# Cross attention: softmax sums taken over keys before the product with the values

## Chip, cores and metric

The program runs on one core of one Trainium2 chip. The metric is the time of one execution on the device in microseconds (us), the median of the runs made; less is better.

## The reference, cut to what matters

The reference is a two-layer network on 2 x 1024 tokens of 256 channels. Two of its parts are cross attentions from the 2048 tokens to 2 x 64 context rows (`ctx_512`), both with 16 heads. The first ("x2" in the kernel) has 32 channels per head:

```
q = einsum('bsc,hcd->bhsd', xn, wq); k = einsum('btc,hcd->bhtd', yn, wk); v = einsum('btc,hcd->bhtd', yn, wv)
a = softmax(einsum('bhsd,bhtd->bhst', q, k) * D ** (-0.5), axis=-1)
o = einsum('bhst,bhtd->bhsd', a, v)
```

The second ("x3") is the same computation with 16 channels per head and biases on q, k and v. Everything else (a self attention, two local attentions, feed-forward parts and a mixture of experts) is outside of the change.

## The kernel before

The program is a sequence of stages, each with its own queues on the engines and a barrier of all engines at its end. Both cross attentions are made by one function, `cross_attention`, which is called with the phase names `x2` and `x3`. It works on 16 tiles of 128 tokens. A tile t passes these steps, and a software pipeline written out by hand (the loops over `it`, one per engine, in each of which the steps stand in a fixed order) decides which steps of which tile stand beside one another:

- `statistics`, `inverse_deviation`, `normalise`, `turn_z`, `inputs`: the layer norm of the tile and its transposition, 10 to 14 tiles ahead. `project` and `queries`: the queries of a group of four tiles, in pieces (4 in x2, 2 in x3), one piece per tile and 6 tiles ahead.
- `score` (TensorE, L1155): all 16 x 64 scores of the 128 tokens into the two banks `sps[t % 2]`. The keys stand in `kblk`, blocked by head.
- `top` (VectorE): the negated maximum over the 64 keys of each head (`nmax`, L983), and the scores less it, written to `prob[:, t % 2, :]` in SBUF (L988).
- `exponent` (ScalarE, L1049): the exponential, in place, 128 x 1024.
- `turn_probs` (TensorE, L1108): eight transpositions of 128 x 128 back into `sps[t % 2]`, so that keys lie on the partitions. `evacuate` (ScalarE, L1044): two copies of 128 x 512 to `pT`.
- `weigh` (TensorE): the product with the values `vblk` into the bank `ops` (L1139), and a product with a matrix `ones` into the bank `dps` (L1143), which gives each head's sum of exponentials, repeated over its channels.
- `outputs` (VectorE): the reciprocal of `dps`, MC x 128 columns wide (512 in x2, 256 in x3, L995), and the product with `ops` into `res` (L998).

In the loops, VectorE's order for an `it` is `outputs(it - 1)`, `top(it + 1)`, `normalise`, `statistics`; ScalarE's is `evacuate(it)`, `exponent(it + 1)`, `inputs`, `queries`; TensorE's is `turn_probs(it)`, `turn_z`, `project`, `weigh(it)`, `score(it + 2)`. `weigh(t)` waits for `out_done` of tile t - 1, since there is one bank `ops`. `score(t)` waits until `evacuate(t - 2)` has emptied the scores' banks.

Of the kernel before, what the change touches and what calls it, by code (L numbers as in the profile page):

```python
# [9 lines left out]
def build(nc, io, out):  # L10
# [6 lines left out]
    ALU = mybir.AluOpType  # L17
# [46 lines left out]
    with stack:  # L64
# [761 lines left out]
        def cross_attention(phase, H, DK, src, res, weights, affine, biases, scale, ahead):  # L826
# [10 lines left out]
            with ExitStack() as c:  # L837
# [8 lines left out]
                vmask = sb(phase + "vmask", [P, 2], F32, c)  # L846
                ones = sb(phase + "ones", [P, 2, DK], F32, c)
                kT = sb(phase + "kT", [P, MC, P], F32, c)
# [13 lines left out]
                pT = sb(phase + "pT", [P, 2, H * CT], F32, c)  # L862
                rinv = sb(phase + "rinv", [P, MC * P], F32, c)
                sps = [ps(f"{phase}s{i}", [P, H * CT], c) for i in range(2)]
                zps = ps(phase + "z_ps", [P, KD * P], c)
                qps = ps(phase + "q_ps", [P, GW], c)
                ops = ps(phase + "o_ps", [P, 512], c)
                dps = ps(phase + "d_ps", [P, 512], c)

                s = signals(phase, "@next_in @filled @cut @masks_done @y_stats @y_moments @y_var @y_rstd @y_done @y_turned "  # L870
                            "@yT_done @ydup_done @kv_made @kT_done @v_done @k_built @v_built @x_stats @x_moments @x_var "
                            "@x_rstd @z_done @z_turned @xT_done @q_done @qT_done @scores @max_done @prob_ready @exp_done "
                            "@p_turned @pT_done @pv_done @rinv_done @out_done")

# [14 lines left out]
                with nc.Block() as block:  # L889
# [5 lines left out]
                    def _(pool):  # L895
# [27 lines left out]
                        pool.wait_ge(s.masks_done, 2)  # L923
                        pool.tensor_copy(ones[:], vmask[:].unsqueeze(2).to_broadcast([P, 2, DK])).then_inc(s.v_built, 1)
                        for t in range(4, 8):
                            inverse_deviation(t)
                        pool.wait_ge(s.v_done, B)
                        for b in range(B):
# [3 lines left out]
                                               ALU.mult).then_inc(s.v_built, 1)  # L932
                        for t in range(8, NT):
                            inverse_deviation(t)

                    @block.vector
                    def _(dve):
# [14 lines left out]
                        def blocks():  # L952
                            dve.wait_ge(s.kv_made, 1)
                            for b, bank in enumerate((ops, dps)):
                                if biases:
                                    dve.tensor_tensor(v[:, b, :], bank[:, 0:W], bv[:], ALU.add).then_inc(s.v_done, 1)
                                else:
                                    dve.tensor_copy(v[:, b, :], bank[:, 0:W]).then_inc(s.v_done, 1)
                            dve.wait_ge(s.masks_done, 2)
                            dve.wait_ge(s.kT_done, MC)  # L960
                            for b in range(B):
                                for m in range(MC):
                                    dve.tensor_tensor(kblk[:, b, m, :, :],
                                                      kT[:, m, b * CT:(b + 1) * CT].unsqueeze(1).to_broadcast([P, HQ, CT]),
                                                      hmask[:].unsqueeze(2).to_broadcast([P, HQ, CT]), ALU.mult).then_inc(s.k_built, 1)
# [26 lines left out]

                        def outputs(t):
                            dve.wait_ge(s.pv_done, t + 1)
                            dve.reciprocal(rinv[:], dps[:, 0:MC * P]).then_inc(s.rinv_done, 1)  # L995
                            dve.wait_ge(s.rinv_done, t + 1)
                            at = t % TPB * P
                            dve.tensor_tensor(res[:, t // TPB * MC:(t // TPB + 1) * MC, at:at + P],  # L998
                                              ops[:, 0:MC * P].rearrange("p (m t) -> p m t", m=MC),
                                              rinv[:].rearrange("p (m t) -> p m t", m=MC), ALU.mult).then_inc(s.out_done, 1)  # L1000

                        for it in range(START, NT + 1):
                            if it == START + 1 and affine:
                                y_norm()
                            if live(it - 1):
                                outputs(it - 1)
                            if live(it + 1):
# [13 lines left out]
                    def _(act):  # L1021
# [25 lines left out]
                        def exponent(t):  # L1047
                            act.wait_ge(s.prob_ready, t + 1)
                            act.activation(prob[:, t % 2, :], prob[:, t % 2, :], ACT.Exp, scale=scale).then_inc(s.exp_done, 1)  # L1049

                        def inputs(t):
                            g, j = t // J, t % J
# [23 lines left out]
                        for it in range(START, NT + 1):  # L1076
                            if live(it):
                                evacuate(it)
                            if live(it + 1):
                                exponent(it + 1)  # L1080
                            if live(it + LEAD_X):
                                inputs(it + LEAD_X)
                            if it == -LEAD_X + 3:
                                keys()
                            if asked(it + LEAD_Q):
                                queries(it + LEAD_Q)

                    @block.tensor
                    def _(pe):
# [5 lines left out]
                        def keys_values():  # L1095
                            pe.wait_ge(s.ydup_done, 1)
                            for m in range(MC):
                                pe.matmul(sps[1][:, m * P:(m + 1) * P], wk[:, m * P:(m + 1) * P], yT[:], start=True, stop=True)
                            for b, bank in enumerate((ops, dps)):
                                mm = pe.matmul(bank[:, 0:W], ydup[:, b, :, :].rearrange("p r t -> p (r t)"), wv[:],  # L1100
                                               start=True, stop=True)
                            mm.then_inc(s.kv_made, 1)

                        def turn_probs(t):
                            pe.wait_ge(s.exp_done, t + 1)
                            for half in range(2):
                                for r in range(half * NP2 // 2, (half + 1) * NP2 // 2):
                                    mm = pe.transpose(sps[t % 2][:, r * P:(r + 1) * P], prob[:, t % 2, r * P:(r + 1) * P], ident[:])  # L1108
                                mm.then_inc(s.p_turned, 1)
# [19 lines left out]
                        def weigh(t):  # L1129
                            b = t // TPB  # L1130
                            pe.wait_ge(s.pT_done, 2 * t + 2)
                            if t == 0:
                                pe.wait_ge(s.v_built, B + 1)
                            else:
                                pe.wait_ge(s.out_done, t)
                            for m in range(MC):
                                for a in range(NC):
                                    r = a * MC + m
                                    pe.matmul(ops[a * WIDE:(a + 1) * WIDE, m * P:(m + 1) * P],  # L1139
                                              vblk[:, b, r, :, :].rearrange("p q d -> p (q d)"),  # L1140
                                              pT[:, t % 2, r * P:(r + 1) * P], start=True, stop=True)
                            for a in range(NC):
                                mm = pe.matmul(dps[a * WIDE:(a + 1) * WIDE, 0:MC * P], ones[:].rearrange("p q d -> p (q d)"),  # L1143
                                               pT[:, t % 2, a * MC * P:(a + 1) * MC * P], start=True, stop=True)
                            mm.then_inc(s.pv_done, 1)
# [1311 lines left out]
```

## Time and profile before

| | before |
|---|---|
| median of three runs | 2368.93 us (2366.84 to 2369.19) |
| the profiled execution | 2361.52 us, of which the profile's span is 2359.7 us |
| TensorE, VectorE, ScalarE, GpSimd busy | 83%, 56%, 43%, 22% of the span |
| x2, from its first subtraction (L988) to its last output (L998) | 109.0 us |
| x3, the same | 80.7 us |

The profile records one execution. Busy shares are averages over all stages; only the two stages of cross attention, some 8% of the span, are touched here, and they are read by themselves.

### The profile page before, as it was taken

How to read it: one execution, taken by the hardware profiler on the slowest of the kernel's cores; microseconds unless marked ns; L12 is line 12 of the kernel's file. 1: busy time of each engine (PE TensorE's matmuls, PEld its weight loads, DVE VectorE, ACT ScalarE, POOL GpSimd, SP SyncE). 2: the span in 40 equal slices, each digit the busy share in tenths (PEclk: the TensorE clock that was granted, in tenths of full speed). 3: DMA queues.
4: the chain of work that ended last, by engine and by line, in shares of the span. 5: the costliest groups of instructions: out<-in, count | busy, mean ns of one | idle time of the engine just before them, and what ended most of it. 6: DMA issues, size and time to landing. Idle time of an engine off the chain costs nothing. (4 is left out here: it accounts for less than half of the span.)

```text
span 2359.7 us, 32440 instructions
## 1 busy us (share of the span) xinstructions
PE 1962.5 (83%) x11804; PEld 1240.0 (53%) x11836; DVE 1318.0 (56%) x2301; ACT 1012.6 (43%) x2111; POOL 528.9 (22%) x893
## 2 busy tenths in 40 slices
PE   3788888888799797896899979979999899874595
PEld 1335555555467465574465655535566455442494
DVE  3548888888623498232666643236666333885412
ACT  1238888888621242211465641116565211432121
POOL 2102222222332300232222210112222110222321
PEclk9889999999999899998999999989999999986797
DMA  2243111110000100002000000030000000027395
GB/s 67 71 132 113 43 39 37 38 37 2 1 1 0 54 1 1 0 1 89 5 1 1 1 1 0 1 105 1 1 1 1 1 1 0 15 56 198 113 308 153
DMA packets 99133, 99.60 MB, mean 42 GB/s; under 512 B 33740, under 2 KB 83232, under 8 KB 98848
## 3 DMA queue, kind: packets, MB, share of 16 engines
q1 hardware_dynamic: 95904, 93.21, 13.2%
q0 software_dynamic: 3072, 4.34, 1.0%
q8 instruction: 94, 1.54, 0.3%
q14 instruction: 63, 0.52, 0.1%
HBM read 80.60 MB, written 16.92 MB: 41 GB/s over the span
## 5 line engine op out<-in xcount | busy, mean ns | idle before, releaser
L515 DVE TENSOR_REDUCE negmax<-sps 128x1 f32<-128x1024 f32 x256 | 307.6, 1212 | 21.6 <-PE sps L466 20.9
L559 ACT ACTIVATE prob<-sps,negmax 128x1024 f32<-128x1024 f32 x256 | 286.2, 1118 | 8.7 <-DVE negmax L515 6.1
L475 PE MATMUL sps<-ident,prob 128*128 128x128 f32 x1152 | 182.2, 287 | 57.0 <-ACT prob L559 56.1
L475 PEld LDWEIGHTS sps<-ident,prob 128*128 128x128 f32 x1152 | 134.7, 144 | 144.2 <-ACT prob L559 129.1
L604 POOL TENSOR_TENSOR probT<-probT,after 128x128 f32<-128x128 f32 x256 | 116.6, 455 | 281.5 <-DVE probT L523 191.3
L466 PE MATMUL sps<-ks,qs 128*128 128x512 f16 x512 | 162.1, 387 | 21.0 <-DVE ores L535 17.7
L568 ACT COPY probT<-sps 128x512 f32<-128x512 f32 (+1 forms) x192 | 101.6, 529 | 22.1 <-PE sps L475 22.1
L1304 POOL TENSOR_TENSOR la1qs<-la1qn,la1sin 128x256 f32<-128x256 f32 x64 | 60.3, 972 | 196.0 <-DVE la1qn L1381 196.0
L1304 POOL TENSOR_TENSOR la0qs<-la0qn,la0sin 128x256 f32<-128x256 f32 x64 | 60.3, 972 | 195.0 <-DVE la0qn L1381 195.0
L523 DVE COPY probT<-sps 128x512 f32<-128x512 f32 (+3 forms) x192 | 91.4, 476 | 4.7 <-PE sps L475 4.7
L491 PE MATMUL sps<-probT,vres 128*32 128x128 f32 x2304 | 82.5, 279 | 8.3 <-POOL probT L604 5.7
L466 PEld LDWEIGHTS sps<-ks,qs 128*128 128x128 f16 x512 | 49.0, 105 | 50.2 <-issue 28.8
L491 PEld LDWEIGHTS sps<-probT,vres 128*32 128x32 f32 x2304 | 58.3, 110 | 26.6 <-POOL probT L604 11.2
L2301 ACT ACTIVATE hTe<-bh,b1e 128x128 f32<-128x128 f32 x128 | 34.7, 382 | 81.6 <-PE bh L2322 81.6
L1549 PE MATMUL la0bqk<-la0w,la0hT 128*128 128x512 f32 x128 | 64.6, 651 | 4.6 <-DVE la0qn L1381 3.8
L1549 PE MATMUL la1bqk<-la1w,la1hT 128*128 128x512 f32 x128 | 64.4, 650 | 4.0 <-DVE la1qn L1381 3.2
L1450 ACT ACTIVATE la1pr<-la1bs,la1nx 128x256 f32<-128x256 f32 x128 | 58.6, 483 | 7.0 <-DVE la1nx L1369 6.8
L1450 ACT ACTIVATE la0pr<-la0bs,la0nx 128x256 f32<-128x256 f32 x128 | 58.6, 483 | 7.0 <-DVE la0nx L1369 6.8
L2322 PEld LDWEIGHTS bh<-xeT,w1e 128*128 128x128 f32 x512 | 60.6, 195 | 0.7
L2322 PE MATMUL bh<-xeT,w1e 128*128 128x128 f32 x512 | 60.7, 278 | 0.0
L795 PE MATMUL t2tps<-t2zT,t2w 128*128 128x512 f32 x128 | 58.5, 617 | 0.9 <-ACT t2zT L760 0.9
L795 PE MATMUL t1tps<-t1zT,t1w 128*128 128x512 f32 x128 | 58.4, 617 | 0.9 <-ACT t1zT L760 0.9
(450 smaller groups left out, 4246.2 us busy)
## 6 DMA issues: line engine op xcount, KB each, us to landing
w1e<-in_fc_T SPq DMA_DIRECT2D x16, 1024.0 KB, 6.6
w2e<-in_fc_T SPq DMA_DIRECT2D x16, 1024.0 KB, 9.6
qs<-q_parts SPq DMA_DIRECT2D x128, 64.0 KB, 1.9
ks<-k_parts SPq DMA_DIRECT2D x128, 64.0 KB, 1.9
q_parts<-parts SPq DMA_DIRECT2D x8, 512.0 KB, 3.6
k_parts<-parts SPq DMA_DIRECT2D x8, 512.0 KB, 5.4
token_rows<-r_row SPq DMA_DIRECT2D x4, 544.0 KB, 3.3
mixed<-r_zero SPq DMA_DIRECT2D x1, 2056.0 KB, 10.8
```

What stands on the lines that cost most here:

```text
L466: mm = pe.matmul(slots[n % 4][:, half * 512:(half + 1) * 512], qs[:, buf, i * P:(i + 1) * P], ks[:, buf, half * 512:(half + 1) * 512], sta ...
L475: mm = pe.transpose(slots[n % 4][:, at * P:(at + 1) * P], prob[:, n % 3, t * P:(t + 1) * P], ident[:])
L491: mm = pe.matmul(acc[j * D1:(j + 1) * D1, 512:512 + P], vres[:, quad * QUAD + j, t, :], probT[:, (tile * QUAD + j) % 6, at * P:(at + 1) * ...
L515: dve.tensor_reduce(negmax[:, n % 4:n % 4 + 1], slots[n % 4][:], X, ALU.max, negate=True).then_inc(s.max_done, 1)
L559: act.activation(prob[:, n % 3, :], slots[n % 4][:], ACT.Exp, bias=negmax[:, n % 4:n % 4 + 1], accum_out=rowsum[:, tile % 2, n % QUAD:n % ...
L568: act.copy(probT[:, n % 6, lo * P:hi * P], slots[n % 4][:, lo * P:hi * P]).then_inc(s.evac_act, 1)
L604: pool.tensor_tensor(blk, blk, after[:], ALU.mult).then_inc(s.masked, 1)
L795: mm = pe.matmul(tps[2 + f % 2][:], w2[:, k, f * P:(f + 1) * P], zT[:, k, :], start=(k == 0), stop=(k == KD - 1))
L1304: pool.tensor_tensor(qs[:, q * HL:(q + 1) * HL, a * 32:(a + 1) * 32], qn[:, q * HL:(q + 1) * HL, (1 - a) * 32:(2 - a) * 32], sinr[:, t % T ...
L1450: ins = act.activation(prob[:, h, :], bs[:, slot(h) * 256:(slot(h) + 1) * 256], ACT.Exp, bias=nmax[:, slot(h):slot(h) + 1], accum_out=rsum ...
L1549: mm = pe.matmul(bqk[:, n * INNER:(n + 1) * INNER], shifted_rows(t, k), wqkv[:, k, n, :], start=(k == 0), stop=(k == KD - 1))
L2322: mm = pe.matmul(bh[e % 2][:, f, :], w1e[:, e % RING, k, f * P:(f + 1) * P], xeT[:, e % 2, k * P:(k + 1) * P], start=(k == 0), stop=(k == ...
```

## The change

The sum over a head's keys is no longer taken by TensorE after the transposition but by VectorE before it, where tokens lie on the partitions: `shares(t)` reduces `prob` (128 x 1024) to 16 sums per token (`total`), takes 16 reciprocals (`rinv`), and multiplies the first half of `prob` (8 heads, 128 x 512) by them in place. GpSimd does the second half (`share`). `turn_probs` waits for each half by itself (`shared0`, `shared1`). The products with `ones` are gone; the free bank makes a second `ops`, and `outputs` becomes a copy by ScalarE. Cut to its core:

```diff
@@ -860,17 +859,17 @@
...
-                rinv = sb(phase + "rinv", [P, MC * P], F32, c)
+                total = sb(phase + "total", [P, 2, H], F32, c)
+                rinv = sb(phase + "rinv", [P, 2, H], F32, c)
...
-                ops = ps(phase + "o_ps", [P, 512], c)
-                dps = ps(phase + "d_ps", [P, 512], c)
+                ops = [ps(f"{phase}o_ps{i}", [P, 512], c) for i in range(2)]
@@ -930,8 +928,18 @@
...
-                        for t in range(8, NT):
+                        def share(t):
+                            pool.wait_ge(s.rinv_done, t + 1)
+                            part = prob[:, t % 2, 512:1024].rearrange("p (h t) -> p h t", h=H // 2)
+                            pool.tensor_tensor(part, part, rinv[:, t % 2, H // 2:H].unsqueeze(2).to_broadcast([P, H // 2, CT]),
+                                               ALU.mult).then_inc(s.shared1, 1)
+
+                        for t in range(8, LEAD_X + AHEAD):
                             inverse_deviation(t)
+                        for t in range(NT):
+                            share(t)
+                            if live(t + LEAD_X + AHEAD):
+                                inverse_deviation(t + LEAD_X + AHEAD)
 
@@ -990,20 +998,24 @@
...
-                        def outputs(t):
-                            dve.wait_ge(s.pv_done, t + 1)
-                            dve.reciprocal(rinv[:], dps[:, 0:MC * P]).then_inc(s.rinv_done, 1)
+                        def shares(t):
+                            dve.wait_ge(s.exp_done, t + 1)
+                            dve.tensor_reduce(total[:, t % 2, :], prob[:, t % 2, :].rearrange("p (h t) -> p h t", h=H),
+                                              X, ALU.add).then_inc(s.totalled, 1)
+                            dve.wait_ge(s.totalled, t + 1)
+                            if t >= 2:
+                                dve.wait_ge(s.shared1, t - 1)
+                            dve.reciprocal(rinv[:, t % 2, :], total[:, t % 2, :]).then_inc(s.rinv_done, 1)
                             dve.wait_ge(s.rinv_done, t + 1)
-                            at = t % TPB * P
-                            dve.tensor_tensor(res[:, t // TPB * MC:(t // TPB + 1) * MC, at:at + P],
-                                              ops[:, 0:MC * P].rearrange("p (m t) -> p m t", m=MC),
-                                              rinv[:].rearrange("p (m t) -> p m t", m=MC), ALU.mult).then_inc(s.out_done, 1)
+                            part = prob[:, t % 2, 0:512].rearrange("p (h t) -> p h t", h=H // 2)
+                            dve.tensor_tensor(part, part, rinv[:, t % 2, 0:H // 2].unsqueeze(2).to_broadcast([P, H // 2, CT]),
+                                              ALU.mult).then_inc(s.shared0, 1)
 
                         for it in range(START, NT + 1):
                             if it == START + 1 and affine:
                                 y_norm()
-                            if live(it - 1):
-                                outputs(it - 1)
+                            if live(it):
+                                shares(it)
                             if live(it + 1):
                                 top(it + 1)
@@ -1047,6 +1059,12 @@
...
+
+                        def outputs(t):
+                            act.wait_ge(s.pv_done, t + 1)
+                            at = t % TPB * P
+                            act.copy(res[:, t // TPB * MC:(t // TPB + 1) * MC, at:at + P],
+                                     ops[t % 2][:, 0:MC * P].rearrange("p (m t) -> p m t", m=MC)).then_inc(s.out_done, 1)
 
@@ -1078,6 +1096,8 @@
...
+                            if live(it - 1):
+                                outputs(it - 1)
@@ -1096,14 +1116,14 @@
...
                         def turn_probs(t):
-                            pe.wait_ge(s.exp_done, t + 1)
                             for half in range(2):
+                                pe.wait_ge(s.shared1 if half else s.shared0, t + 1)
                                 for r in range(half * NP2 // 2, (half + 1) * NP2 // 2):
                                     mm = pe.transpose(sps[t % 2][:, r * P:(r + 1) * P], prob[:, t % 2, r * P:(r + 1) * P], ident[:])
                                 mm.then_inc(s.p_turned, 1)
@@ -1130,18 +1150,15 @@
...
                             pe.wait_ge(s.pT_done, 2 * t + 2)
                             if t == 0:
-                                pe.wait_ge(s.v_built, B + 1)
-                            else:
-                                pe.wait_ge(s.out_done, t)
+                                pe.wait_ge(s.v_built, B)
+                            if t >= 2:
+                                pe.wait_ge(s.out_done, t - 1)
                             for m in range(MC):
                                 for a in range(NC):
                                     r = a * MC + m
-                                    pe.matmul(ops[a * WIDE:(a + 1) * WIDE, m * P:(m + 1) * P],
-                                              vblk[:, b, r, :, :].rearrange("p q d -> p (q d)"),
-                                              pT[:, t % 2, r * P:(r + 1) * P], start=True, stop=True)
-                            for a in range(NC):
-                                mm = pe.matmul(dps[a * WIDE:(a + 1) * WIDE, 0:MC * P], ones[:].rearrange("p q d -> p (q d)"),
-                                               pT[:, t % 2, a * MC * P:(a + 1) * MC * P], start=True, stop=True)
+                                    mm = pe.matmul(ops[t % 2][a * WIDE:(a + 1) * WIDE, m * P:(m + 1) * P],
+                                                   vblk[:, b, r, :, :].rearrange("p q d -> p (q d)"),
+                                                   pT[:, t % 2, r * P:(r + 1) * P], start=True, stop=True)
                             mm.then_inc(s.pv_done, 1)
```

The first place where the order of instructions moves is VectorE's queue in x2, in the tiles behind the last layer norm. Before (`x2s0` and `x2s1` are the scores' banks, `x2nmax` the maxima, `x2d_ps` and `x2o_ps` the banks `dps` and `ops`):

```order
L988 TENSOR_TENSOR x2prob<-x2s0,x2nmax 128x1024 [waits x2_p_turned,x2_max_done]
L995 RECIPROCAL x2rinv<-x2d_ps 128x512 [waits x2_pv_done]
L998 TENSOR_TENSOR ores<-x2o_ps,x2rinv 128x4x128 [waits x2_rinv_done]
L983 TENSOR_REDUCE x2nmax<-x2s1 128x16 [waits x2_scores]
L988 TENSOR_TENSOR x2prob<-x2s1,x2nmax 128x1024 [waits x2_p_turned,x2_max_done]
```

and in the changed kernel (`x2total` holds the 16 sums):

```order
L996 TENSOR_TENSOR x2prob<-x2s0,x2nmax 128x1024 [waits x2_p_turned,x2_max_done]
L1003 TENSOR_REDUCE x2total<-x2prob 128x16 [waits x2_exp_done]
L1008 RECIPROCAL x2rinv<-x2total 128x16 [waits x2_shared1,x2_totalled]
L1011 TENSOR_TENSOR x2prob<-x2prob,x2rinv 128x512 [waits x2_rinv_done]
L991 TENSOR_REDUCE x2nmax<-x2s1 128x16 [waits x2_scores]
L996 TENSOR_TENSOR x2prob<-x2s1,x2nmax 128x1024 [waits x2_p_turned,x2_max_done]
```

A tile had four VectorE instructions, two of them after `weigh`; it now has five, three of them between the exponential and the transpositions, and the maximum of the next tile stands behind these three.

The second place is TensorE's queue in x2, a tile that has a projection but no layer norm (`x2q_ps` is the projection's bank). Before:

```order
L1108 MATMUL x2s0<-ident,x2prob 128x128 [waits x2_exp_done]
L1108 MATMUL x2s0<-ident,x2prob 128x128 x7
L1125 MATMUL x2q_ps<-x2xT,x2wq 128x512 [waits x2_qT_done,a1p_v_done]
L1125 MATMUL x2q_ps<-x2xT,x2wq 128x512
L1139 MATMUL x2o_ps<-x2pT,x2vblk 64x128 [waits x2_out_done,x2_pT_done]
L1139 MATMUL x2o_ps<-x2pT,x2vblk 64x128 x7
L1143 MATMUL x2d_ps<-x2pT,x2ones 64x512 x2
L1155 MATMUL x2s0<-x2kblk,x2qT 128x256 [waits x2_pT_done,x2_qT_done]
L1155 MATMUL x2s0<-x2kblk,x2qT 128x256 x3
```

and in the changed kernel:

```order
L1128 MATMUL x2s0<-ident,x2prob 128x128 [waits x2_shared0]
L1128 MATMUL x2s0<-ident,x2prob 128x128 x3
L1128 MATMUL x2s0<-ident,x2prob 128x128 [waits x2_shared1]
L1128 MATMUL x2s0<-ident,x2prob 128x128 x3
L1145 MATMUL x2q_ps<-x2xT,x2wq 128x512 [waits x2_qT_done,a1p_v_done]
L1145 MATMUL x2q_ps<-x2xT,x2wq 128x512
L1159 MATMUL x2o_ps0<-x2pT,x2vblk 64x128 [waits x2_out_done,x2_pT_done]
L1159 MATMUL x2o_ps0<-x2pT,x2vblk 64x128 x7
L1172 MATMUL x2s0<-x2kblk,x2qT 128x256 [waits x2_pT_done,x2_qT_done]
L1172 MATMUL x2s0<-x2kblk,x2qT 128x256 x3
```

The product with `x2ones` is gone, the transpositions of a tile wait twice, and `weigh` writes to two banks in turn.

## Rows read from the trace of the kernel before

**Rows 1.** The page of the profile, its head: the span

```profile
span 2359.7 us, 32440 instructions
```

**Rows 2.** Timeline of x2, one tile: start us, us, engine, line, operation, names

```profile
873.78 0.69 DVE L998 TENSOR_TENSOR ores<-x2o_ps,x2rinv 128x512 f32<-128x512 f32 x1
874.39 1.22 DVE L983 TENSOR_REDUCE x2nmax<-x2s 128x16 f32<-128x1024 f32 x1
875.64 1.22 DVE L988 TENSOR_TENSOR x2prob<-x2s,x2nmax 128x1024 f32<-128x1024 f32 x1
876.78 3.35 DVE L995 RECIPROCAL x2rinv<-x2d_ps 128x512 f32<-128x512 f32 x1
876.90 1.06 ACT L1049 ACTIVATE x2prob<-x2prob 128x1024 f32<-128x1024 f32 x1 [3.18 <-DVE x2prob L988]
878.49 1.04 PE L1108 MATMUL x2s<-ident,x2prob 128*128 128x128 f32 x8
879.13 1.07 ACT L1044 COPY x2pT<-x2s 128x512 f32<-128x512 f32 x2 [0.70 <-PE x2s L1108]
879.36 1.88 PE L1125 MATMUL x2q_ps<-x2xT,x2wq 128*128 128x512 f32 x4
881.18 1.09 PE L1139 MATMUL x2o_ps<-x2pT,x2vblk 128*64 128x128 f32 x16
882.10 1.03 PE L1143 MATMUL x2d_ps<-x2pT,x2ones 128*64 128x512 f32 x4
```

**Rows 3.** Timeline of x2, the first scores and the last tile

```profile
825.98 1.89 PE L1155 MATMUL x2s<-x2kblk,x2qT 128*128 128x256 f32 x8
827.91 1.22 DVE L983 TENSOR_REDUCE x2nmax<-x2s 128x16 f32<-128x1024 f32 x1 [5.14 <-PE x2s L1155]
829.17 1.22 DVE L988 TENSOR_TENSOR x2prob<-x2s,x2nmax 128x1024 f32<-128x1024 f32 x1
...
926.73 1.22 DVE L988 TENSOR_TENSOR x2prob<-x2s,x2nmax 128x1024 f32<-128x1024 f32 x1
937.47 0.69 DVE L998 TENSOR_TENSOR ores<-x2o_ps,x2rinv 128x512 f32<-128x512 f32 x1
```

**Rows 4.** Timeline of x3, first and last subtraction, last output

```profile
2026.67 1.22 DVE L988 TENSOR_TENSOR x3prob<-x3s,x3nmax 128x1024 f32<-128x1024 f32 x1
...
2099.18 1.22 DVE L988 TENSOR_TENSOR x3prob<-x3s,x3nmax 128x1024 f32<-128x1024 f32 x1
2099.25 0.64 PE L1139 MATMUL x3o_ps<-x3pT,x3vblk 128*32 128x128 f32 x16 [0.73 <-ACT x3pT L1044]
2106.96 0.42 DVE L998 TENSOR_TENSOR ores<-x3o_ps,x3rinv 128x256 f32<-128x256 f32 x1
```

**Rows 5.** By source line: duration in ns, minimum/median/maximum, over SBUF and 16 columns

```profile
L1364 DVE TENSOR_REDUCE la0ss<-la0sq x16: 1219/1220/1221, 1118.4 to 1361.9; 128x16 f32<-128x1024 f32 x16
...
L1377 DVE RECIPROCAL la0rn<-la0rn x16: 252/252/253, 1120.1 to 1365.5; 128x16 f32<-128x16 f32 x16
```

**Rows 6.** By tile: the block products that VectorE makes while GpSimd works

```profile
L963 DVE TENSOR_TENSOR x2kblk<-x2kT,x2hmask x8: 412/414/1262, 815.7 to 819.7; 128x256 f32<-128x256 f32 x8
...
L963 DVE TENSOR_TENSOR x3kblk<-x3kT,x3hmask x4: 678/889/1101, 2016.4 to 2019.1; 128x512 f32<-128x512 f32 x4
```

**Rows 7.** Timeline of x2, set-up: VectorE copy, GpSimd block products

```profile
815.11 0.68 DVE L958 COPY x2v<-x2d_ps 128x512 f32<-128x512 f32 x1
815.87 2.33 POOL L929 TENSOR_TENSOR x2vblk<-x2v,x2vmask 128x512 f32<-128x512 f32 x2 [7.29 <-DVE x2v L958]
```

**Rows 8.** Busy by stretch: PE, PEld, DVE, ACT, POOL; then PEclk

```profile
2080.00:2090.00 10.00, 7.89 (x74) 4.42 (x72) 9.83 (x9) 5.08 (x8) 0.00 (x0) 1.00 0.00 1
...
932.85:936.27 3.42, 1.19 (x11) 0.31 (x6) 2.19 (x1) 0.00 (x0) 0.00 (x0) 1.00 0.02 5
936.27:939.68 3.41, 0.56 (x2) 0.50 (x3) 1.86 (x2) 0.00 (x0) 0.58 (x1) 0.50 0.00 0
```

**Rows 9.** Timeline of x2, set-up: two matmuls of 512 columns

```profile
811.23 1.91 PE L1100 MATMUL x2d_ps<-x2wv,x2ydup 128*128 128x512 f32 x2
```

More of the change, by code:

```diff
@@ L846, in cross_attention @@
                 vmask = sb(phase + "vmask", [P, 2], F32, c)
-                ones = sb(phase + "ones", [P, 2, DK], F32, c)
                 kT = sb(phase + "kT", [P, MC, P], F32, c)
@@ L872, in cross_attention @@
                             "@x_rstd @z_done @z_turned @xT_done @q_done @qT_done @scores @max_done @prob_ready @exp_done "
-                            "@p_turned @pT_done @pv_done @rinv_done @out_done")
+                            "@p_turned @pT_done @pv_done @totalled @rinv_done @shared0 @shared1 @out_done")
                 def live(t):
@@ L923, in _ @@
                         pool.wait_ge(s.masks_done, 2)
-                        pool.tensor_copy(ones[:], vmask[:].unsqueeze(2).to_broadcast([P, 2, DK])).then_inc(s.v_built, 1)
                         for t in range(4, 8):
@@ L953, in blocks @@
                             dve.wait_ge(s.kv_made, 1)
-                            for b, bank in enumerate((ops, dps)):
+                            for b, bank in enumerate(ops):
                                 if biases:
@@ L1098, in keys_values @@
                                 pe.matmul(sps[1][:, m * P:(m + 1) * P], wk[:, m * P:(m + 1) * P], yT[:], start=True, stop=True)
-                            for b, bank in enumerate((ops, dps)):
+                            for b, bank in enumerate(ops):
                                 mm = pe.matmul(bank[:, 0:W], ydup[:, b, :, :].rearrange("p r t -> p (r t)"), wv[:],
```

## Prediction

> **What bounds the kernel now.** The page's head gives the span, 2359.7 us [rows 1], in an execution of 2361.52. Its busy shares mix all stages, so I went to the timeline of each cross attention. In x2 a tile is VectorE's alone: output product at 873.78, maximum 874.39, subtraction 875.64, next reciprocal 876.78, which takes 3.35 [rows 2]. VectorE comes round after 0.61 + 1.25 + 1.14 + 3.39 = 6.39 us and never waits. TensorE has work for less, and of that the product with ones is 1.03 [rows 2]. In x3 the reciprocal is half as wide, and a tile takes (2099.18 - 2026.67) / 15 = 4.83 us on average [rows 4]. From first subtraction to last output x2 takes 937.47 + 0.69 - 829.17 = 108.99 and x3 2106.96 + 0.42 - 2026.67 = 80.71 [rows 3, 4]. These two numbers are what the change can move.
>
> **What it removes and adds.** Removed per tile: the wide reciprocal and output product on VectorE, the product with ones on TensorE. Added: a sum over 1024 elements from SBUF (1.22, as the 16-column sum of L1364), a reciprocal of 16 columns (0.25, L1377) [rows 5], a VectorE product of 128x512 with both inputs in SBUF (0.68 alone, the minimum of x3kblk) [rows 6], a GpSimd product of that size, and a ScalarE copy of at most half of 1.07 or so [rows 2], which stands behind the exponential, in time when ScalarE waits for VectorE.
>
> **The new ring.** On VectorE alone that is less work than before in x2, 1.26 + 0.29 + 0.61 + 1.25 + 1.22 = 4.6 us. But `shares(t + 1)` needs the exponential of t + 1, which needs `top(t + 1)`, which stands directly ahead of it in VectorE's queue. So VectorE now waits out each exponential. Start to start: exponential to sum 1.06 + 0.04 (a hand-over, as subtraction end 876.86 to 876.90) [rows 2]; sum to reciprocal 1.22 + 0.04; reciprocal to product 0.25 + 0.04 [rows 5]; product to maximum 0.61; maximum to subtraction 1.25; subtraction to exponential 1.26 [rows 2]. Sum: 1.10 + 1.26 + 0.29 + 0.61 + 1.25 + 1.26 = **5.77 us per tile**, the same in x2 and x3, because both have 16 heads of 64 keys. Layer-norm work of the early tiles falls into the wait for the exponential and costs nothing.
>
> **GpSimd's half.** Its price is not in the trace as such. The nearest is the block product of the same size, 2.33 us for two, 1.17 each, recorded while VectorE made its own [rows 7]. Of VectorE's eight, most took 0.41 and at most some 1.26 [rows 6]: one waited 0.85 for the other engine. So GpSimd's own work is between 0.85 and 1.17; I take 1.0. It is released by the reciprocal's end as VectorE's product is; GpSimd started 815.11 + 0.68 to 815.87 = 0.08 after its releaser [rows 7], VectorE starts 0.04 after, so I let VectorE go first. The Trainium skill, "SBUF — State Buffer", section "SBUF: two separate sides", says the same of the lock: a VectorE instruction with two SBUF inputs and a GpSimd one that reads SBUF exclude each other for a whole instruction; by that rule, the trace agrees (1.26 against 0.41). From the reciprocal's start: product 0.29, GpSimd from 0.90 to 1.90, transposition of the second half 1.92, copy 0.64 later, 0.53 long, then the exponential at 3.09. VectorE's own way there is 0.29 + 0.61 + 1.25 + 1.26 = 3.41. GpSimd is covered by 0.3 us.
>
> **TensorE's chain over two tiles.** It is not covered where a projection stands. From a reciprocal's start: 1.92, four transpositions 0.44, projection 1.82, `weigh` 0.92 [rows 2], scores to maximum 1.93 [rows 3], then 1.25 + 1.26 + 1.10 + 1.26 to the reciprocal two tiles on: 11.90 against 2 x 5.77 = 11.54. In x2 projections stand in tiles 0 to 9 (six ahead), and in tiles 0 to 5 two more transpositions, 0.22: three pairs at +0.58, two at +0.36, 2.5 in all. Without a projection the chain waits for the copy instead (1.92 + 0.64 + 0.54 = 3.10, then 0.92 + 1.93 + 4.87 = 10.82), slack 0.7. In x3 `weigh` takes 0.64 [rows 4] in place of 1.09, and a projected pair, 11.4, fits.
>
> **Sums.** x2: 15 x 5.77 + 2.5 = 89.0; tail from the last subtraction 1.26 + 1.10 + 1.26 + 1.92 + 0.64 + 0.58 + 1.1 (`weigh`, with its way out) + 0.6 (copy) = 8.5, where before it was 938.16 - 926.73 = 11.4 [rows 3]. 97.5 against 108.99: **-11.5**. x3: 86.55 + 7.8 (`weigh` 0.45 and the copy, half as wide, 0.25 shorter) = 94.35 against 80.71: **+13.6**. Together +2.1; with GpSimd at 0.85 +1.1, at 1.17 +3.4.
>
> **TensorE's clock** is the last term. In x3 TensorE was busy 7.89 of 10 us at full clock; at x2's drained end it was busy 1.19 of 3.41, and the next stretch was granted 0.50 [rows 8]. In the new ring its work per tile without projection is transpositions 1.04 [rows 2], scores 1.89 [rows 3] and in x3 a `weigh` of 0.64 [rows 4], 3.6 of 5.77 us, in lumps: after the scores it rests 1 us or more, then has two half-transpositions with a gap, a gap, `weigh`. Such poor stretches recur every tile, so I expect some falls to 1.2 GHz in x3 and late x2. Each doubles what it meets: two 512-column matmuls took 1.91 at x2's start, where four take 1.88 [rows 2, 9]. A fall over one tile's transpositions, `weigh` and scores adds up to 0.4 + 0.9 + 1.8 to a chain with 0.7 to 1.1 slack, so nothing to 2.4; I take four falls at 1.0, **+4**, between 0 and 10. Total +2.1 + 4 = **+6.1 us**. The profiled execution lies 7.4 below the median of the runs; the same shift taken for both kernels, the median becomes 2368.93 + 6.1 = **2375**.
>
> **Rivals.** A) *The clock holds.* Then +1.1 to +3.4: 2370 to 2372. For it: before, x2 stayed at full clock between tiles without projection. Against: there the product with ones filled in. 0.22. B) *GpSimd gets the port first.* Its product starts before VectorE's and VectorE's waits 0.85 to 1.04 in each of 30 ring turns: +25 to +31 more, less some 1 for an earlier second half: 2396. It speaks for it that in x2kblk VectorE did lose one turn to GpSimd [rows 6]; against it the 0.04 lead. The page named above says that issue order decides; by that rule, this is the case in which GpSimd's wake-up is quicker than VectorE's wait for its own reciprocal. 0.12. C) *Not slower: the drained ends are cheaper.* x2's new tail is 3 us shorter and has no 3.35 us of reciprocal under which TensorE rests, so the clock need not fall there [rows 3, 8]; the next stage would start at full clock and save half of the 3.4 us that it spent at 0.50, in x3 alike. If the ring also keeps the clock: 2.1 - 3.4, and with the ring 0.1 shorter per tile another -3: 2365 to 2368. It decides from ring turns under 5.65 us. 0.10. D) *GpSimd's product is much longer*, 1.6 or more, as an in-place product with a broadcast input may be. The ring through GpSimd passes 3.41 at a product of 1.32 us; at 1.6, 0.28 x 30 = 8.4 more and 0.6 on each chained pair: 2386. 0.08. That the change does not do what it says is excluded by the order of instructions.
>
> **How the numbers follow.** The forecast (ring of 5.77, a few clock falls) gets the remaining 0.48, its own range is 2370 to 2382. What a measurement of this kernel can tell from no change is about 0.2%, 4.7 us. Of the forecast about a sixth lies under +4.7, A is wholly within, C is half faster, B and D are slower; a further allowance of some 5 in 100 is for runs of the two kernels that differ by chance, as the 7.4 us above warn. Faster 0.10, same 0.31, slower 0.59. The range from 2364 to 2390 leaves out B and the lower edge of C.
>
> **What would show it.** VectorE's idle time ahead of `x2total` and `x3total` should be the exponential's, about 1.1 us a tile, released by ScalarE; the subtractions should follow at 5.8 us in both stages, 6.0 where x2 projects; VectorE's product of 128x512 should be near 0.68, GpSimd's near 1.0 to 1.6 as recorded (with its wait); x2 should take about 98 and x3 about 95 us, plus what the clock takes; the stretches of x3 should show a granted clock under 1.00. Wrong it would be if VectorE's product reads 1.5 us (B), if the exponential is released by ScalarE's own copies (D), or if x3 stays near 81.

## Result and the profile after

The changed kernel takes 2378.16 us (median of five runs, 2376.92 to 2379.34), the kernel before 2366.84 (now five runs, 2364.98 to 2369.19); the ratio is 1.0047, with a 95% interval of 1.0032 to 1.0061. It is slower by 11 us. The profiled execution took 2377.62 us, its span is 2375.8.

The two stages by themselves, from the first subtraction to the last output, in a view of busy time by stretch (x2, then x3; TensorE, its weight loads, VectorE, ScalarE, GpSimd; the last columns are the granted clock, the DMA share and GB/s):

```profile
822.86:924.19 101.33, 86.61 (x558) 59.18 (x556) 75.21 (x91) 53.34 (x89) 27.14 (x22) 0.96 0.00 1
2013.59:2114.50 100.91, 75.30 (x474) 37.87 (x472) 75.19 (x91) 44.30 (x76) 27.15 (x22) 0.90 0.00 1
```

The same view of the kernel before:

```profile
829.17:938.16 108.99, 93.35 (x622) 61.81 (x620) 103.63 (x75) 43.68 (x73) 2.36 (x6) 0.99 0.00 1
2026.67:2107.38 80.71, 69.36 (x602) 38.78 (x600) 74.40 (x75) 38.73 (x60) 2.37 (x6) 0.98 0.00 1
```

x2 went from 108.99 to 101.33 us and x3 from 80.71 to 100.91 us [rows 3, 4]. Together that is +12.54. VectorE's busy time in x2 fell from 103.63 to 75.21 us: it no longer fills the stage, and yet the ring through its queue sets the pace in most turns. In x3 VectorE is about as busy as before (75.19 against 74.40) and the stage is 20 us longer. TensorE's mean granted clock in x3 is 0.90, where it was 0.98; 1.00 stands for 2.4 GHz and 0.50 for 1.2 GHz. In the kernel before, the clock falls only in the tails of the two stages (from 936.3 and 2103.6), not in their loops.

A stretch of the timeline of x2, with a projection in each tile, to be read against [rows 2] (start, duration, engine, line, operation):

```profile
870.04 1.99 PE L1172 MATMUL x2s<-x2kblk,x2qT 128*128 128x256 f32 x8
870.53 0.25 DVE L1008 RECIPROCAL x2rinv<-x2total 128x16 f32<-128x16 f32 x1
870.82 0.69 DVE L1011 TENSOR_TENSOR x2prob<-x2prob,x2rinv 128x512 f32<-128x512 f32 x1
870.86 1.55 POOL L934 TENSOR_TENSOR x2prob<-x2prob,x2rinv 128x512 f32<-128x512 f32 x1 [4.21 <-DVE x2rinv L1008]
872.07 1.23 DVE L991 TENSOR_REDUCE x2nmax<-x2s 128x16 f32<-128x1024 f32 x1 [0.56 <-PE x2s L1172]
872.51 1.24 ACT L1056 COPY x2pT<-x2s 128x512 f32<-128x512 f32 x2 [2.30 <-PE x2s L1128]
872.96 1.88 PE L1145 MATMUL x2q_ps<-x2xT,x2wq 128*128 128x512 f32 x4
873.33 1.22 DVE L996 TENSOR_TENSOR x2prob<-x2s,x2nmax 128x1024 f32<-128x1024 f32 x1
874.59 1.06 ACT L1061 ACTIVATE x2prob<-x2prob 128x1024 f32<-128x1024 f32 x1 [0.84 <-DVE x2prob L996]
874.77 0.85 PEld L1159 LDWEIGHTS x2o_ps<-x2pT,x2vblk 128*64 128x64 f32 x16 [0.76 <-issue]
875.68 1.22 DVE L1003 TENSOR_REDUCE x2total<-x2prob 128x16 f32<-128x1024 f32 x1 [1.12 <-ACT x2prob L1061]
875.80 1.59 PEld L1172 LDWEIGHTS x2s<-x2kblk,x2qT 128*128 128x128 f32 x8 [0.17 <-issue]
876.94 0.25 DVE L1008 RECIPROCAL x2rinv<-x2total 128x16 f32<-128x16 f32 x1
877.83 1.22 DVE L991 TENSOR_REDUCE x2nmax<-x2s 128x16 f32<-128x1024 f32 x1
```

From one reciprocal (870.53) to the next (876.94) it takes 6.41 us and the next turn again 5.75 (882.69, not shown). VectorE's sum starts only 1.09 us after the exponential: 874.59 to 875.68. The maximum at 872.07 waited 0.56 for TensorE's scores (870.04), the one at 877.83 started right behind VectorE's own product. So turns of the ring on VectorE alternate with turns in which TensorE's chain over two tiles is the longer one. The gaps between the 16 subtractions of x2 are 5.75, 7.81, 5.75, 6.62, 5.76, 6.62, 5.76, 6.40, 5.76, 6.40, 5.76, and four of 5.75; those of x3 are 5.75 except for 7.64, 7.74, 5.95, 6.62 and 6.62.

The two halves of the product, by tile in x3 (duration in ns, minimum/median/maximum; in the last line, GpSimd's idle time in us that the reciprocal ended, in 16 tiles):

```profile
L1011 DVE TENSOR_TENSOR x3prob<-x3prob,x3rinv x16: 691/692/694, 2017.5 to 2109.5; 128x512 f32<-128x512 f32 x16
L934 POOL TENSOR_TENSOR x3prob<-x3prob,x3rinv x16: 1547/1548/1550, 2017.5 to 2109.6; 128x512 f32<-128x512 f32 x16
...
  DVE x3rinv L1008: 61.3, 16
```

GpSimd's is recorded with 1.55 us, VectorE's of the same size with 0.69, and GpSimd's starts 0.04 after VectorE's (870.82 and 870.86).

What lies outside of the two stages runs the same code and varies by itself. x2's first subtraction came at 829.17 before and 822.86 after; from x3's last output to the end it took 252.3 us before and 261.3 after. The experiments below show either value of each (829.15 and 252.1 in the second, 823.45 and 261.3 in the fifth). So I compare the stages in the profile, and whole times only by ratios from one chip. In the experiments, the time behind "against" is the median of the kernel before, run beside the experiment on the same chip.

### The profile page after: what moved, and what is told of

It is laid out like the page before. It is cut to its first block and busy times, and to the rows that moved or that the text cites. A ratio compares the mean times of both kernels' runs of the same rounds, so it can differ in the third digit from the quotient of the medians.

```text
span 2375.8 us, 32210 instructions
## 1 busy us (share of the span) xinstructions
PE 1962.4 (83%) x11644; PEld 1235.6 (52%) x11644; DVE 1290.9 (54%) x2333; ACT 1028.0 (43%) x2143; POOL 579.1 (24%) x923
## 5 line engine op out<-in xcount | busy, mean ns | idle before, releaser
L2348 PE MATMUL by<-w2e,hTe 128*128 128x256 f32 x256 | 60.4, 387 | 4.6 <-issue 4.6
```

## Experiments

**1 and 2. The change in one stage alone.** The other stage calls the function as it was before, kept under a second name:

```diff
-        cross_attention("x3", H3, D3, lambda t: xres[:, t, :], ores, x3_weights, False, biases3, D3 ** -0.5, router_ahead)
+        cross_attention_old("x3", H3, D3, lambda t: xres[:, t, :], ores, x3_weights, False, biases3, D3 ** -0.5, router_ahead)
```

(in the second experiment the same for `"x2"`).

Change in x2 alone. 

> The change in x2 alone, x3 as before. Theory 1 (each stage changes by its own ring, 5.75 us a tile in both): x2 takes about 101 us from first subtraction to last output, x3 81, so the whole is 7 to 8 us faster than before, about 2359. Rival (the 11 us lie in something both stages or the stages behind them share, such as when other transfers run): half of the loss, 4 to 6 us slower than before.

Change in x3 alone. 

> The change in x3 alone, x2 as before. Theory 1: x3 takes about 100 us instead of 81, the whole 18 to 20 us more than before, about 2386. Rival (shared cause): 4 to 6 us more than before.

Measured: x2 alone 2352.63 us against 2358.8, ratio 0.9974 (0.9961 to 0.9987); x3 alone 2379.31 (four runs), ratio 1.0074 (1.0053 to 1.0096). In the profiles the changed stage takes 101.39 and 100.12 us, the unchanged one 80.69 and 108.99. The first one by stretch:

```profile
824.25:925.64 101.39, 86.68 (x558) 59.14 (x556) 75.20 (x91) 53.34 (x89) 27.14 (x22) 0.96 0.00 1
2014.95:2095.64 80.69, 69.35 (x602) 38.75 (x600) 74.39 (x75) 38.73 (x60) 2.37 (x6) 0.98 0.00 1
```

That is -6.1 and +17.5 us by the ratios, and their sum, +11.4, is the whole change (+11.1) within the intervals, which are 3 and 5 us wide to either side. The loss is x3's and the gain x2's: each stage takes the same time, to 0.8 us, whether the other is changed or not. Both effects by the ratios are a little smaller than expected (7 to 8 and 18 to 20).

**3. Halves.** The subtraction, the exponential and the sum are each cut into two instructions over 8 heads, with their signals counted by halves:

```diff
 in top(t)
-                            dve.tensor_tensor(prob[:, t % 2, :].rearrange("p (h t) -> p h t", h=H),
...
+                            for half in range(2):
+                                q, hh = slice(half * 512, half * 512 + 512), slice(half * H // 2, (half + 1) * H // 2)
+                                dve.tensor_tensor(prob[:, t % 2, q].rearrange("p (h t) -> p h t", h=H // 2),
...
 in exponent(t)
-                            act.wait_ge(s.prob_ready, t + 1)
-                            act.activation(prob[:, t % 2, :], prob[:, t % 2, :], ACT.Exp, scale=scale).then_inc(s.exp_done, 1)
+                            for half in range(2):
+                                q = slice(half * 512, half * 512 + 512)
+                                act.wait_ge(s.prob_ready, 2 * t + half + 1)
+                                act.activation(prob[:, t % 2, q], prob[:, t % 2, q], ACT.Exp, scale=scale).then_inc(s.exp_done, 1)
 in shares(t)
-                            dve.wait_ge(s.exp_done, t + 1)
-                            dve.tensor_reduce(total[:, t % 2, :], prob[:, t % 2, :].rearrange("p (h t) -> p h t", h=H),
...
+                            for half in range(2):
+                                q, hh = slice(half * 512, half * 512 + 512), slice(half * H // 2, (half + 1) * H // 2)
+                                dve.wait_ge(s.exp_done, 2 * t + half + 1)
+                                dve.tensor_reduce(total[:, t % 2, hh], prob[:, t % 2, q].rearrange("p (h t) -> p h t", h=H // 2),
...
```

> The changed kernel in both stages, with the subtraction, the exponential and the sum each cut into two halves of 8 heads, so that VectorE's sum of the first half runs under ScalarE's exponential of the second. Theory 1 (VectorE waits out each exponential, 1.12 us a tile): the ring falls from 5.75 to about 5.0, pairs with a projection from 12.4 to 11.4 us, both stages together 15 to 22 us less than in the changed kernel, about 2358. Rival (GpSimd's product and ScalarE's copies behind it hold the exponential back): the ring stays within 0.2 us of 5.75, and the four more instructions a tile make it slightly slower, 2378 to 2382.

Measured: 2353.62 us, ratio to before 0.9979 (0.9966 to 0.9991), so 5 us faster than before the change, with both stages changed. x2 takes 95.08 and x3 89.25, together 17.9 less than in the changed kernel. (It has three more instructions a tile, not four as the expectation says.) A turn in x3 and the start of the next, by the timeline:

```profile
2070.98 1.28 DVE L1007 TENSOR_REDUCE x3total<-x3prob 128x8 f32<-128x512 f32 x2 [0.34 <-ACT x3prob L1067]
2072.29 0.25 DVE L1012 RECIPROCAL x3rinv<-x3total 128x16 f32<-128x16 f32 x1
2072.58 0.69 DVE L1015 TENSOR_TENSOR x3prob<-x3prob,x3rinv 128x512 f32<-128x512 f32 x1
2073.19 1.22 DVE L991 TENSOR_REDUCE x3nmax<-x3s 128x16 f32<-128x1024 f32 x1
2074.44 1.29 DVE L998 TENSOR_TENSOR x3prob<-x3s,x3nmax 128x512 f32<-128x512 f32 x2
2074.92 0.59 ACT L1060 COPY x3pT<-x3s 128x512 f32<-128x512 f32 x1 [0.31 <-PE x3s L1134]
2075.40 1.15 ACT L1067 ACTIVATE x3prob<-x3prob 128x512 f32<-128x512 f32 x2
2076.07 1.28 DVE L1007 TENSOR_REDUCE x3total<-x3prob 128x8 f32<-128x512 f32 x2 [0.34 <-ACT x3prob L1067]
```

The two pairs of sums stand 5.09 us apart (2070.98 and 2076.07). The wait of VectorE for the exponential is 0.34 a tile instead of 1.12. Pairs of turns with a projection take 11.3 us late in x2 instead of 12.16. Not all of the gain is the ring's: in x3 the clock falls once, early (2013.5 to 2020.3), and not again before the tail, and its mean is 0.95 instead of 0.90. The exponential (2075.40) now starts behind ScalarE's second copy (2074.92), although the first half of the subtraction was done near 2075.1 (estimated as half of the 1.29). So what the prediction's fourth rival named, ScalarE's copies, looks like the next bound here; this is read from the timeline, and no run tests it.

**4. Filling TensorE's rest.** In tiles without projection, a few matmuls without use go to the projection's bank behind the scores:

```diff
                                 score(it + LEAD_S)
+                                if it >= 0 and not asked(it + LEAD_Q):
+                                    pe.wait_ge(s.qT_done, sum(asked(n) for n in range(it + LEAD_Q + 1)))
+                                    for _ in range(4 if MC == 2 else 3):
+                                        pe.matmul(qps[:, 0:256], ident[:], kblk[:, 0, 0, 0:4, :].rearrange("p q t -> p (q t)"),
+                                                  start=True, stop=True)
```

> The changed kernel with three (x2) or four (x3) matmuls of 256 columns without use, put behind the scores of each tile that has no projection, where TensorE rests. Theory 1 (the gaps over 5.75 us outside of the projected pairs come from the clock's falls): the gaps of 7.8, 7.7, 6.6 us lose 0.9 to 2 us each and the granted clock of x3 goes from 0.90 to 0.97 or more, the two stages 5 to 8 us shorter, about 2371. Rival (the gaps are waits of another kind and the filling delays the transpositions): same gaps, time 2378 or more.

Measured: 2369.02 us against 2358.8, ratio 1.0035 (1.0024 to 1.0047); the changed kernel without filling has 1.0047.

```profile
829.31:931.03 101.72, 90.19 (x582) 64.14 (x580) 75.19 (x91) 52.65 (x89) 27.13 (x22) 0.96 0.00 1
2020.15:2119.45 99.30, 84.88 (x554) 52.02 (x552) 74.99 (x91) 42.99 (x76) 27.13 (x22) 0.94 0.00 1
```

x3's granted clock is 0.94 instead of 0.90, where 0.97 was expected. Its gaps of 6.62 are gone (late gaps 5.75 to 5.89), and in the loop only the early fall is left (2025.2 to 2032.0). That the late gaps come with falls is borne out by two more executions of the same x3 stage, experiments 2 and 7: each has one late fall (2107.0 and 2078.3) where the changed kernel has two, and each has one gap of 6.62, over that fall.

The early gaps are less clear. The first, 7.62, stayed, as did 7.85 in x2, where the early tiles have projections and are not filled; both still have a fall over them. The pair of 5.75 and 7.74 became 6.37 and 6.54 with no fall over it: of the 1.99 over the ring, 0.58 went with the fall. The rest stands beside filling matmuls, behind which the transpositions now start (fillers at 2032.06 and 2037.94), so this run does not show how much of it the fall had caused.

x3 gained 1.6 us against the 100.91 of the changed kernel, and 0.8 against the 100.12 and 100.14 of experiments 2 and 7, less than the 5 to 8 expected for the two stages; x2 gained nothing (101.72). The intervals of the two ratios overlap, so the whole times do not show a gain. The mechanism holds for the late gaps; its size this run does not show.

**5. The best of both.** x2 as in experiment 3, x3 as before the change. 

> x2 with the change and the three steps cut in halves, x3 as before. Theory (stage times add up): x2 95 us, x3 81 us, together 14 us less than before; ratio to before 0.994. Rival (part of what the halves gained came from x3's earlier end or from the stages behind): ratio 0.997 or more.

Measured: 2354.36 us against 2366.53, ratio 0.9948 (0.9934 to 0.9963), with 95.10 and 80.81 us in the stages. By the ratios it is 12 us faster than the kernel before and 23 us faster than the changed one. The ratio expected was 0.994.

**6. Both halves of the product on VectorE.**

```diff
 in shares(t)
-                            if t >= 2:
-                                dve.wait_ge(s.shared1, t - 1)
...
-                            part = prob[:, t % 2, 0:512].rearrange("p (h t) -> p h t", h=H // 2)
...
+                            for half, done in enumerate((s.shared0, s.shared1)):
+                                part = prob[:, t % 2, half * 512:half * 512 + 512].rearrange("p (h t) -> p h t", h=H // 2)
+                                dve.tensor_tensor(part, part, rinv[:, t % 2, half * H // 2:(half + 1) * H // 2].unsqueeze(2)
+                                                  .to_broadcast([P, H // 2, CT]), ALU.mult).then_inc(done, 1)
 in GpSimd's loop
-                            share(t)
```

> The changed kernel with both halves of the product on VectorE and none on GpSimd. Theory 1 (VectorE's ring is what binds, GpSimd is covered): the ring grows by the second product, 5.75 to 6.3 or 6.4 us a tile, while the pairs with a projection (12.4 us) hardly grow; two stages 10 to 15 us longer than in the changed kernel. Rival (GpSimd's product, 1.55 us as recorded, holds the second half up): the transpositions come 0.3 us sooner and the ring stays or shrinks.

Measured (two runs): 2386.14 us against 2366.53, ratio 1.0078 (1.0055 to 1.0101). x2 takes 105.99 and x3 104.09, together 7.8 more than in the changed kernel, where 10 to 15 were expected. One turn in x2:

```profile
903.28 0.25 DVE L1005 RECIPROCAL x2rinv<-x2total 128x16 f32<-128x16 f32 x1
903.57 1.29 DVE L1009 TENSOR_TENSOR x2prob<-x2prob,x2rinv 128x512 f32<-128x512 f32 x2
904.78 1.22 DVE L990 TENSOR_REDUCE x2nmax<-x2s 128x16 f32<-128x1024 f32 x1
906.03 1.23 DVE L995 TENSOR_TENSOR x2prob<-x2s,x2nmax 128x1024 f32<-128x1024 f32 x1
907.29 1.06 ACT L1059 ACTIVATE x2prob<-x2prob 128x1024 f32<-128x1024 f32 x1 [1.09 <-DVE x2prob L995]
```

From exponential (900.94, one turn earlier) to exponential it is 6.35 us, and all 30 gaps but one (7.19) are 6.35 or 6.36. The ring grew by the 0.60 of the second product, as VectorE's ring demands. The total grew less than 30 x 0.60, since the pairs with a projection disappeared under the longer ring, and x3 lost nothing to its clock in the loop although the clock fell there twice (2021.9 and 2079.9).

**7. A memset ahead of GpSimd's product.**

```diff
+                            pool.memset(idle[:], 0.0)
                             part = prob[:, t % 2, 512:1024].rearrange("p (h t) -> p h t", h=H // 2)
```

> The changed kernel with a memset of 128x512 by GpSimd (about 0.5 us, writes to an unused tensor) between its release and its product. Theory 1 (of the 1.55 us recorded for GpSimd's product, some 0.65 are a wait for VectorE's product, which holds the port): the memset runs under that wait, the product is recorded with 1.0 to 1.1 us and ends when it did, 1.9 us after the reciprocal's start; gaps as in the changed kernel. Rival (the product itself takes 1.55 us): it ends 0.5 us later, the pairs with a projection grow from 12.4 to 12.9 us, and the ring passes 5.75.

Measured (a single run): 2380.1 us, stages of 101.38 and 100.14 us. The gaps are those of the changed kernel to 0.1 us, but for one gap of 6.62 in x3 instead of two.

```profile
872.04 0.25 DVE L1010 RECIPROCAL x2rinv<-x2total 128x16 f32<-128x16 f32 x1
872.35 0.52 POOL L934 MEMSET x2idle<- 128x512 f32 x1 [4.19 <-DVE x2rinv L1010]
872.83 1.08 POOL L936 TENSOR_TENSOR x2prob<-x2prob,x2rinv 128x512 f32<-128x512 f32 x1
```

The product is now recorded with 1.08 us, in x3 too, and ends 1.87 us after the reciprocal's start (872.83 + 1.08 - 872.04), where in the changed kernel it was 870.86 + 1.55 - 870.53 = 1.88. Half a microsecond of extra GpSimd work cost nothing in the gaps. So at least 0.47 of the recorded 1.55 is a wait that lies under VectorE's product.

## Why the prediction came out as it did

The forecast was +6.1 us and a median of 2375, in the range of 2364 to 2390; measured were 2378.16 us, +11.1 by the ratio and +12.5 in the stages. The direction, the place (x2 gains, x3 loses) and the ring held; two terms of the sum were too small, and the effect is nearly twice the forecast. That the median came within 3 us of 2375 is partly luck: the base of 2368.93 from three runs became 2366.84 with five.

**The ring of 5.77 us** is 5.75 in both stages. Shown by the gaps, by experiment 6 (0.60 more on VectorE makes 0.60 more a turn) and by experiment 3 (covering part of the exponential takes 0.66 off it). Its steps, read in the timeline of x3 below: exponential to sum 1.08 (predicted 1.10), sum to reciprocal 1.26, reciprocal to product 0.29, product to maximum 0.60, maximum to subtraction 1.26, subtraction to exponential 1.26.

**GpSimd's half.** The product was taken at 1.0 and its end at 1.90 after the reciprocal's start; it is 1.88. The order was right as well: VectorE's product is 0.69 in all 32 tiles, never 1.5, so rival B fell. The Trainium skill ("SBUF — State Buffer", section "SBUF: two separate sides") says that whichever of the two instructions starts first has the shared port for its whole length and the other is blocked; the trace agrees, and experiment 7 shows the wait: its length shrinks by what is put ahead of it. From VectorE's recorded end (870.82 + 0.69 = 871.51) to GpSimd's (872.41) it is 0.90, nearer to the lower bound of 0.85 than to the 1.0 taken. The end came out right because two errors cancel: VectorE's product ended 0.98 after the reciprocal's start and not 0.90, and GpSimd's was 0.10 shorter.

**TensorE's chain over two tiles** was put at 11.90 with a projection and 12.12 with two more transpositions. Measured: 6.40 + 5.76 = 12.16 and 6.62 + 5.76 = 12.38. What was too small are the prices: `weigh` to scores takes 1.03 (874.77 to 875.80), not 0.92, scores to maximum 2.03 (870.04 to 872.07), not the 1.93 read at a rested engine, and the second four transpositions 0.50, not 0.44. Five pairs with 0.26 and the shorter ring make x2 1.2 us longer than predicted. In x3 "a projected pair fits" was wrong by the same prices: the late pair with a projection takes 5.75 + 5.95 = 11.70 against 11.50, with no fall over it, and its maximum waits for the scores. With the two more transpositions of the early tiles it would be 12.38 - 0.45 = 11.93, an estimate from x2's pair.

**TensorE's clock** was the term with the wrong size: +4 was taken, between 0 and 10, and it is some 8.6 by the count below. The timeline of x3 around a fall:

```profile
2073.02 0.25 DVE L1008 RECIPROCAL x3rinv<-x3total 128x16 f32<-128x16 f32 x1
2073.31 0.69 DVE L1011 TENSOR_TENSOR x3prob<-x3prob,x3rinv 128x512 f32<-128x512 f32 x1
2073.91 1.22 DVE L991 TENSOR_REDUCE x3nmax<-x3s 128x16 f32<-128x1024 f32 x1
2074.95 0.42 PEld L1128 LDWEIGHTS x3s<-ident,x3prob 128*128 128x128 f32 x4 [0.48 <-POOL x3prob L934]
2075.17 1.23 DVE L996 TENSOR_TENSOR x3prob<-x3s,x3nmax 128x1024 f32<-128x1024 f32 x1
...
2076.28 0.38 PEld L1159 LDWEIGHTS x3o_ps<-x3pT,x3vblk 128*32 128x32 f32 x16 [0.91 <-ACT x3pT L1056]
2076.43 1.06 ACT L1061 ACTIVATE x3prob<-x3prob 128x1024 f32<-128x1024 f32 x1 [0.19 <-DVE x3prob L996]
2076.94 0.50 PEld L1172 LDWEIGHTS x3s<-x3kblk,x3qT 128*128 128x128 f32 x2 [0.28 <-issue]
2076.94 3.55 PE L1172 MATMUL x3s<-x3kblk,x3qT 128*128 128x512 f32 x4
2077.51 1.22 DVE L1003 TENSOR_REDUCE x3total<-x3prob 128x16 f32<-128x1024 f32 x1 [1.12 <-ACT x3prob L1061]
...
2080.33 1.04 PE L1128 MATMUL x3s<-ident,x3prob 128*128 128x128 f32 x8
2080.53 1.23 DVE L991 TENSOR_REDUCE x3nmax<-x3s 128x16 f32<-128x1024 f32 x1 [0.78 <-PE x3s L1172]
2081.79 1.23 DVE L996 TENSOR_TENSOR x3prob<-x3s,x3nmax 128x1024 f32<-128x1024 f32 x1
```

and the same three stretches by busy time (granted clock third from the end):

```profile
2073.30:2076.70 3.40, 1.73 (x24) 1.21 (x24) 3.05 (x3) 1.45 (x3) 1.55 (x1) 1.00 0.02 5
2076.70:2080.10 3.40, 3.40 (x14) 1.36 (x5) 2.17 (x3) 1.04 (x2) 1.00 (x1) 0.50 0.00 0
2080.10:2083.50 3.40, 2.67 (x27) 1.65 (x26) 2.45 (x2) 1.53 (x3) 0.55 (x1) 1.00 0.00 0
```

TensorE was busy half of the first stretch (1.73 of 3.40 us), then was granted 0.50, and the four matmuls of the scores took 3.55 us instead of the 1.98 of the tile before. The maximum behind them waited 0.78 and the gap became 6.62: +0.87.

The falls in the loops are five, where four were assumed. The two late ones, both in x3, cost 0.87 each. The three early ones stand over the gap of 7.64 in x3 (+1.89), that of 7.74 in x3 (+1.99) and that of 7.81 in x2 (+1.19 over the 6.62 of its kind). Of the 1.99, some 0.4 would be there without a fall, by the estimate of 11.93 above. That makes 6.4 us in the loops. The two tails, 9.94 and 8.84 instead of 8.5 and 7.8, have a fall too, which was not priced at all: four transpositions took 1.11 instead of 0.66 in both, and `weigh` 1.98 instead of 1.09 in x2 and 1.08 instead of 0.64 in x3, together 2.2. So the step of the prediction that fell short is the price of a fall, taken at 1.0: it is 0.87 late, 1.2 to 1.9 early, 0.9 and 1.3 in the tails.

Put together: 2.1 as predicted without the clock, 1.2 for x2's pairs, 0.3 for x3 (0.6 for its pairs with a projection, less 0.3 for the shorter ring), 8.6 for the clock and 0.3 for other steps of the tails are 12.5 of the 12.54 measured.

That a fall causes the gap is shown for the late ones: they come and go together in the four executions whose x3 has the ring of 5.75 (two in the changed kernel, one each in experiments 2 and 7, none in experiment 4). For the early gaps and the tails it is read from the trace only, from the doubled durations of TensorE's pieces.

**Rivals.** A, the clock holds, is refuted by x3's 0.90 and the five falls in the loops. C, a shorter tail of x2 spares the next stage its slow start, is refuted: x2's tail is 1.5 us shorter only, and the clock stood at 0.50 from 919.6. D, GpSimd's product so long that the exponential waits behind ScalarE's copies, is refuted for the change, whose ring is 5.75 with a product of at most 1.08 behind VectorE's; its wait shows in the version with halves, because VectorE's way became shorter there.

**The median.** The prediction moved the profile's time by 7.4 us to the median. For the changed kernel profile and median agree within 0.6 us, and the medians of the kernel before measured with the result and the experiments run from 2358.8 to 2366.84. So the offset is not a fixed property of the kernel; whether it comes from the chip or from the execution no run separates.

## What to carry to other kernels

When work is moved between engines, write out the ring of waits in the order in which each engine's queue holds its steps, and not the busy sums: here VectorE got less to do in x2 and still set the pace, since it had to wait out an exponential that, in the late tiles, nothing of its own covered. One function that serves two shapes should be costed for both: what removed a 512-column reciprocal in one stage removed one of half that width in the other, and paid the same ring. A step that several engines hand round can be cut in halves so that one half's hand-over lies under the other half's work.

## Not expected of the hardware

A GpSimd instruction was recorded with 1.55 us of which at least 0.47 is a wait for VectorE's instruction: it is recorded with 1.08 when it starts later, behind a memset. TensorE's clock fell inside a steady loop in which TensorE worked 75.30 of 100.91 us. A loop of longer turns (experiment 6, 6.35 us) met four falls and paid for at most one of them, the first of x2, which stands over its gap of 7.19.
